# A transformer decoder layer on one core: the loop over the sequences with six of them in its body instead of one

## What is computed

```python
x = x + attn(layernorm(x), Wq, Wk, Wv, Wo)                  # 16 heads of 64, rotary embedding, no mask
x = x + xattn(layernorm(x), ctx, mask, Wq, Wkv, Wout, bout) # 16 heads of 64, keys and values from ctx
x = x + ffn(layernorm(x), Wg, We, be)                       # 8 experts 256x256, top 2 by softmax gates
```

## Time and profile before

| | us |
|---|---|
| median of 3 executions (3658.17 to 3659.45) | 3658.52 |
| the profiled execution, its own time | 3660.11 |
| its span (first to last instruction) | 3658.2 |
| TensorE busy in the span | 3508.1 (96%) |
| VectorE busy | 2357.1 (64%) |
| ScalarE busy | 2232.2 (61%) |
| GpSimd busy | 2123.2 (58%) |
| mean granted TensorE clock | 0.993 of full speed |

### The profile page before, as it was taken

The page is one execution under the profiler, slowest core; times in us unless marked ns, Lnnn a source line. Parts: engine busy times, 40 slices in busy tenths (PEclk is TensorE's granted clock), DMA queues, the critical chain, the costliest instruction groups (busy, mean ns, idle before and its releaser), DMA issues.

```text
span 3658.2 us, 87217 instructions
## 1 busy us (share of the span) xinstructions
PE 3508.1 (96%) x28992; PEld 2956.4 (81%) x28992; DVE 2357.1 (64%) x7401; ACT 2232.2 (61%) x6442; POOL 2123.2 (58%) x1928
## 2 busy tenths in 40 slices
PE   5999999999999999999999999999999999999997
PEld 4788888888888888888888888888888888888886
DVE  6666666666666666666666666666666666666665
ACT  5656566665565665666655655656666566556563
POOL 5555666555665556665556655566655566555661
PEclk8999999999999999999999999999999999999999
DMA  3100000000000000000000000000000000000000
GB/s 96 37 10 12 13 7 10 10 12 12 7 12 11 10 12 11 9 10 10 12 12 7 10 10 13 12 10 10 10 10 12 12 7 10 10 12 12 10 9 7
DMA packets 46845, 48.23 MB, mean 13 GB/s; under 512 B 8256, under 2 KB 43328, under 8 KB 46400
## 3 DMA queue, kind: packets, MB, share of 16 engines
q1 hardware_dynamic: 45696, 41.99, 3.9%
q10 hardware_dynamic: 704, 0.27, 0.0%
HBM read 33.86 MB, written 8.39 MB: 12 GB/s over the span
## 4 chain that ended last, share of the span: by engine, by line
PE 44%; issue 33%; POOL 16%; DVE 4%; ACT 2%; POOLq 0%; DMA 0%; ACTq 0%; DVEq 0%
PE unit_ps L537 10%; POOL probs L1147 10%; PE oT_ps L666 7%; PE pT_ps L649 7%; PE score_ps L633 7%; PE unit_ps L525 5%; PE wo_ps L691 4%; POOL rope L1159 2%; POOL swap L1155 2%; POOL q_both L1136 1%; ACT probs L800 1%; PE unit_ps L556 1%; DVE neg_max L928 1%; POOL rstd L1123 1%; PE unit_ps L547 1%
## 5 line engine op out<-in xcount | busy, mean ns | idle before, releaser
L1147 POOL TENSOR_TENSOR probs<-probs,inv_sum 128x512 f32<-128x512 f32 x1024 | 1062.1, 1041 | 1007.6 <-DVE inv_sum L922 1006.6
L789 ACT ACTIVATE pT<-pT_ps 128x512 f32<-128x512 f32 x1024 | 608.8, 596 | 146.8 <-PE pT_ps L649 144.6
L800 ACT ACTIVATE probs<-probs,neg_max 128x256 f32<-128x256 f32 x1024 | 510.9, 502 | 268.9 <-DVE probs L939 268.9
L649 PE MATMUL pT_ps<-ident,probs 128*128 128x128 f32 x4096 | 637.9, 281 | 11.1 <-POOL probs L1147 10.7
L649 PEld LDWEIGHTS pT_ps<-ident,probs 128*128 128x128 f32 x4096 | 452.8, 141 | 224.2 <-issue 152.6
L800 ACT ACTIVATE probs<-score_ps,neg_max 128x256 f32<-128x256 f32 x1024 | 477.9, 477 | 218.6 <-DVE neg_max L928 218.6
L666 PE MATMUL oT_ps<-pT,v_sb 128*64 128x256 f32 x4096 | 560.8, 395 | 4.5 <-ACT pT L789 4.1
L939 DVE TENSOR_SCALAR_CACHE_REDUCE probs<-score_ps,mask_add 128x256 f32<-128x256 f32 x1024 | 433.3, 479 | 104.2 <-PE score_ps L633 102.3
L537 PE MATMUL unit_ps<-xs_hi,w_lo 128*128 128x256 f32 x1536 | 460.5, 300 | 9.2 <-DVE swap L973 7.7
L537 PE MATMUL unit_ps<-xs_hi,w_hi 128*128 128x256 f32 x1536 | 436.7, 284 | 0.0
L537 PE MATMUL unit_ps<-xs_lo,w_hi 128*128 128x256 f32 x1536 | 436.3, 284 | 0.0
(11 more groups left out here) (121 smaller groups left out, 8528.0 us busy)
## 6 DMA issues: line engine op xcount, KB each, us to landing
x_in<-dram_x SPq DMA_DIRECT2D x32, 256.0 KB, 2.7
xn<-dram_ctx SPq DMA_DIRECT2D x32, 256.0 KB, 2.7
layer_out<-x SPq DMA_DIRECT2D x32, 256.0 KB, 2.2
swap<-dram_bout SPq DMA_DIRECT2D x32, 128.0 KB, 3.0
rope<-dram_be SPq DMA_DIRECT2D x32, 64.0 KB, 2.8
rope<-dram_we SPq DMA_DIRECT2D x5, 256.0 KB, 2.7
probs<-dram_sk SPq DMA_DIRECT2D x4, 256.0 KB, 4.3
x<-dram_cq SPq DMA_DIRECT2D x4, 256.0 KB, 3.1
```

The source lines that it names most:

```text
L649: last = nc.tensor.transpose(pT_ps[s % 2][:, k * T + t * P:k * T + (t + 1) * P], probs[:, hs % P_BUFS, t, k * P:(k + 1) * P], ident[:])
L789: nc.scalar.activation(flat(pT[:, s % 2, :, :]), pT_ps[s % 2][:], ACT.Copy).then_inc(pT_ready.sem, 1)
L800: last = nc.scalar.activation(dst, src, ACT.Exp, bias=neg_max[:, h % STATS, t:t + 1], scale=1.0 if h < H else -1.0, accum_out=row_sum[:, h ...
L1147: nc.gpsimd.tensor_tensor(weights, weights, inv.unsqueeze(2).to_broadcast([P, NT, T]), ALU.mult).then_inc(probs_ready.sem, 1)
```

## The change

The loop steps by six, and its body holds six bodies in a row, for b, b+1, ... b+5. It makes five turns. Nothing else is changed; line numbers behind the new lines grow by four or five.

```diff
+TURNS = 6
+assert (B - 2) % TURNS == 0
+
+
 def bias_first(s):
...
             body(-1)
             body(0)
-            with engine.Fori(1, B - 1) as b:
-                body(b)
+            with engine.Fori(1, B - TURNS, TURNS) as b:
+                for n in range(TURNS):
+                    body(b + n)
             body(B - 1)
             body(B)
```

## The result

The changed kernel takes 3605.97 us (median of 4 executions, 3604.93 to 3608.12), the kernel before 3658.98 us on the same chip (3658.17 to 3660.6). The ratio is 0.9855, with a 95% interval of 0.9838 to 0.9872: 53 us less. The forecast was 3608 us, range 3600 to 3624.

A forecast was written before the change was run, and what follows sets the result against it. TensorE's work plus its gaps was taken to bound the kernel. The profiled 3660.1 - 52.0 + 1.2 gave 3609.3 us; the median of the runs lies 1.6 us lower, so 3607.7, rounded to 3608 us, range 3600 to 3624.

The forecast's parts named there:

- Term 1: Seams between loop turns: 25 of 29 become straight code, each saving 2.25 us before a correction.
- Term 2: Body 31's constants explain 0.17 us of its shorter period, leaving 2.08 us per seam, 52.0 us for 25.
- The cross-check's clock drops: Half-clock stretches behind idle seams: six fall to an expected 0.8, giving back 8.8 us; with the gaps 52.2 us.
- Term 3: At the four seams that keep the branch, ScalarE and GpSimd may now stand: 0.3 us each, 1.2 us added.
- The sign named for it: Issue waits of ScalarE and GpSimd, with a count of four, would show their pauses at the remaining branched seams.
- the term's high end: ScalarE and GpSimd stand 2.3 us, as VectorE does, at each of the four branched seams: 9.2 us added.
- Term 4: Longer straight code inside the loop, newly streamed on GpSimd and ScalarE: taken to cost nothing.
- A: Clock drops have another cause and stay, only seam gaps go: gain 42.2 us, 3616 us; chance 12%.
- B: Time saved at seams half returns inside the body as TensorE waits for probabilities: 3632 us; chance 6%.
- C: The seam's wait for GpSimd is real and the branch costs next to nothing: stays at 3658 us; chance 3%.
- D: GpSimd and ScalarE stand at every code block in the longer loop: 234 us added, 3842 us; chance 2%.

The follow-up runs named there:

- the near branches: Changed kernel with a tiny two-turn loop at each of its 25 straight seams, on all five engines: 3607.13 us, ratio 0.9843 to the kernel before.
- the runs with pauses: Changed kernel with 48, 72 or 100 satisfied waits in TensorE's stream at each of the 25 straight seams: 3626.57, 3684.92 and 3761.42 us.
- TensorE alone: Kernel before with six bodies in TensorE's loop only, the other four engines still branching back after each sequence: 3635.8 us, ratio 0.9915.

## Why the prediction was right

1. **Term 1, 25 seams, 2.25 us less a correction.** Right. The gaps fell to the four forecast, with VectorE's beside them. The seam's price taken from the single unbranched seam of the kernel before held for the 25 new ones: 2.14 us by the periods, 2.08 forecast. That the gap is the fetch of code behind the branch, which the prediction argued, the packets and the near branches show.
2. **Term 2, the constants.** Right in sign and nearly in size. Body 31's 0.17 us was to make the straight period 109.86; it is 109.80, so the correction was 0.11. The 25 x 0.06 = 1.5 us are half of what the forecast missed. (With thirty bodies, constants throughout a body gave 0.09 us; so not all of the 0.11 in 20 slots need be theirs.)
3. **The cross-check's clock drops.** The mechanism was argued from six coincidences; the runs with pauses show it. Its size was off by chance: 0.8 drops expected at the four seams, none in the profile, 1.4 us. The other profiles with four branched seams and no added waits had none to three.
4. **Term 3, ScalarE and GpSimd at the four seams, 1.2 us.** The four branched periods in the profile exceed 109.80 by 7.8 us in all, the four gaps are 7.0 us; so at most 0.8 us lies there, and the run without these two engines' six bodies can't tell it from zero. The sign named for it, issue waits with a count of four, isn't in the lists, yet both engines stand, for some 3 us each time, nearly as long as VectorE. So the condition of the term's high end (9.2 us) came true and its price did not: the pause stands beside VectorE's own.
5. **Term 4, straight code, nothing.** Right: 114 packets more on queue 14 at no measurable cost, and 109.80 us period after period.

The sum was 3609.3 us against the profiled execution, which took 3606.3: 1.5 and 1.4 us of the 3.0 are in points 2 and 3, and the second of these is luck.

Where the text was too simple: "VectorE stands too, but beside TensorE's gap" is true of the change but suggests that VectorE's pause is free. Without TensorE's gap it is the next wait, 0.98 us per seam (as TensorE alone showed; the rival there had 1.4). And the price of a branched seam is no constant: with two bodies its gap is 2.17 us instead of 1.73, mostly because of where the code lies.

The rivals: A (drops from another cause) fell with the pauses; B (the gain comes back inside the body) didn't happen with both engines straight, but its mechanism is real, as TensorE alone showed; C (a true wait for GpSimd, a cheap branch) fell, though its second half is right for near code: 25 such branches on each engine added 0.03 us to a period. The Trainium skill (Advanced Engine Details and Errata, Control Flow Timing) gives some 108 ns for a compare-and-branch, a figure for the branch and not for the code behind it; TensorE's records here have 0.08 us for one that falls through, 0.21 to 0.35 us for one to near code and 3.3 us and more for one whose target is fetched. D (ScalarE and GpSimd stand at every piece of code) didn't happen; they stand only behind a branch.

## What to carry to other kernels

Price a loop's back edge from the trace: the count of a gap (turns minus one) finds it, and a seam that falls through gives the price with restart and clock in it. Unroll the engine that bounds the kernel and those it soon waits for: TensorE alone gained 31 us here, TensorE and VectorE 56, the other three added nothing, and all four without TensorE gained nothing. A wait's named releaser is the last event and need not be the cause; a place in the same program where the order is the same and the wait is absent tells which it is.

## What the runs showed of the hardware

- After the taken branch at the end of the loop TensorE's sequencer was held 3.3 to 3.9 us in the kernel before (up to 4.6 with two bodies), with a 16 KB packet of code behind each; its array stood 1.5 to 2.7 us, and VectorE 2.2 us and more by issue. To a target a few instructions back neither stood.
- Short loops did not stand: ScalarE with 202 listed instructions and GpSimd with 108 went on 0.24 and 0.26 us after the branch, and so did GpSimd with two bodies (about 214). ScalarE with two bodies (about 400), GpSimd with six (638) and VectorE with one (270) stood some 3 us.
- The idle time behind such a branch depends on where the code lies: 2.13 us in the mean, 1.81 us with the code moved by 64 instructions. It was long where another packet of code was on its way at the branch.
- A satisfied wait in TensorE's stream takes about 0.054 us of its issuing: 24 more lengthened the gap from 0.63 to 1.9 us, 28 more to 3.5. By that price 48 waits take 2.6 us, so about the first 2 us of such a pause were hidden (an estimate), by matmuls already issued.
- Idle stretches of 0.63 us at full load never dropped the clock (0 of 25), those of 1.9 us did so in 13 of 25, those of 3.5 us in 22 of 25. The clock then stood at 0.50 (1.2 GHz) for 3.4 us or 6.8 us.
- The kernel before had 6 clock drops on one chip, and the kernel with as many branched seams on TensorE 12 on another. The kernel before ranged from 3659 to 3676 us over the chips, the one with six bodies from 3606 to 3611 over two.
